# mLSTM stage of a fused kernel: a third score bank, one vector step behind each head, block maxima begun in the first stage, and no block of its own for the constants

## The reference

```python
q = layernorm(x);  k = v = ctx                          # 4 batches x 512 positions x 512
ig = cat(q,k,v) @ Wi + bi;  fg = cat(q,k,v) @ Wf + bf   # 16 gates of each kind per position
F = cumsum(log_sigmoid(fg));  log_D[s,t] = F[s] - F[t] + ig[t] for t <= s, else -inf
D = exp(log_D - rowmax(log_D))
C = (q_h @ k_h.T / sqrt(32)) * D                        # per head of 32 features, 512 x 512
h = (C / (max(|sum C|, exp(-rowmax)) + 1e-6)) @ v_h
x = x + tanh(g) * headwise_layernorm(h) * ln_scale
```

## Time and profile before

| | us |
|---|---|
| runs shown: median of 3 (lowest, highest) | 1750.79 (1750.56, 1753.29) |
| profiled execution, its own time | 1748.16 |
| its span | 1746.4 |
| PE busy in the span | 1389.4 |
| DVE busy | 1243.4 |
| ACT busy | 767.4 |
| POOL busy | 321.9 |

### The profile page before, as it was taken

How to read it: one execution, slowest core, us unless ns; L and a number is a source line. 1 busy time by engine, 2 the same in 40 slices (tenths; PEclk the granted TensorE clock), 3 DMA queues, 4 the chain that set the end, 5 groups by cost and what they waited for, 6 DMA issues and landing times. The chain is left out here.

```text
span 1746.4 us, 24792 instructions
## 1 busy us (share of the span) xinstructions
PE 1389.4 (80%) x9060; PEld 788.7 (45%) x9060; DVE 1243.4 (71%) x1952; ACT 767.4 (44%) x1450; POOL 321.9 (18%) x233
## 2 busy tenths in 40 slices
PE   3589899735568798987487696877999999999997
PEld 2367677521233344433354464533444444444443
DVE  4354666676256777895799999858778877788764
ACT  2433444335334354432688797823333333333322
POOL 0021142244555455754000000000000000000000
PEclk9777888755789899999798798989999999999998
DMA  7012133214533324222503000000000000000000
GB/s 254 3 51 71 61 121 97 73 53 149 146 101 98 117 89 129 85 98 101 200 2 120 24 0 0 0 1 4 9 6 6 6 12 6 6 6 6 12 6 12
DMA packets 56494, 102.19 MB, mean 59 GB/s; under 512 B 9823, under 2 KB 20727, under 8 KB 56300
## 3 DMA queue, kind: packets, MB, share of 16 engines
q1 hardware_dynamic: 55148, 97.14, 17.1%
q0 software_dynamic: 1280, 4.20, 0.9%
HBM read 73.47 MB, written 27.66 MB: 58 GB/s over the span
## 5 line engine op out<-in xcount | busy, mean ns | idle before, releaser
L2047 PE MATMUL HG<-W1H,XT 128*128 128x512 f16 x512 | 166.7, 388 | 27.2 <-ACT XT L2008 20.7
L1521 PE MATMUL FD<-W0D,HH 128*128 128x512 f16 x512 | 159.2, 394 | 14.6 <-DMA W0D<-down_weights,IDX 11.0
L2047 PE MATMUL HU<-W1H,XT 128*128 128x512 f16 x512 | 163.2, 380 | 0.0
L2073 PE MATMUL HD<-W1H,HT 128*128 128x512 f16 x512 | 155.3, 380 | 0.0
L1515 PE MATMUL FG<-F,W0G 97*128 97x512 f16 x324 | 84.4, 394 | 49.8 <-DMA F<-features_kept 23.3
L318 ACT ACTIVATE DD<-E,TM 128x128 f32<-128x128 f32 x256 | 72.6, 370 | 115.8 <-PE E L411 115.6
L1768 ACT ACTIVATE PR<-A_S,NM,CM 128x512 f32<-128x512 f32 x128 | 99.5, 777 | 34.4 <-DVE NM L1909 34.4
L2016 ACT ACTIVATE SG<-HG,DS 128x512 f32<-128x512 f32 x64 | 43.9, 686 | 160.3 <-PE HU L2047 160.3
L2150 DVE SCALAR_TENSOR_TENSOR H<-HU,DS,SG 128x512 f32<-128x512 f32 x64 | 48.0, 750 | 87.4 <-ACT SG L2016 85.4
L1405 POOL TENSOR_TENSOR HL<-HM,HH 128x512 f16<-128x512 f32 x64 | 92.5, 1445 | 82.6 <-ACT HH L1444 82.0
L1521 PE MATMUL FD<-W0D,HL 128*128 128x512 f16 x256 | 100.8, 394 | 0.0
(11 more groups left out here) (333 smaller groups left out, 3376.7 us busy)
## 6 DMA issues: line engine op xcount, KB each, us to landing
VALP<-in_ffn_weights_dram SPq DMA_DIRECT2D x24, 512.0 KB, 3.5
VALQ<-in_ffn_weights_dram SPq DMA_DIRECT2D x24, 512.0 KB, 3.6
quantised_weights<-QQ SPq DMA_DIRECT2D x24, 512.0 KB, 2.8
X<-in_x_dram SPq DMA_DIRECT2D x8, 1024.0 KB, 6.2
CTX<-in_ctx_dram SPq DMA_DIRECT2D x8, 1024.0 KB, 5.5
W1H<-quantised_weights SPq DMA_DIRECT2D x3, 2048.0 KB, 10.5
W1L<-quantised_weights SPq DMA_DIRECT2D x3, 2048.0 KB, 15.2
F<-features_kept SPq DMA_DIRECT2D x16, 288.0 KB
```

The lines of the kernel that those rows point to most:

```text
L1521: last = pe.matmul(DN[c][:, :], lhs[:, i, c * P:(c + 1) * P], W2[:, i, part, :], start=(i == 0 and n == 0), stop=(i == KI - 1 and n == 2))
L2047: ins = pe.matmul(bank[:, :], lhs, rhs, start=(i == 0), stop=(i == len(terms) - 1))
L2073: ins = pe.matmul(DN[0][:, :], HT[:, q, lp, k, :], W[:, 2, i * D:(i + 1) * D], start=(i == 0 and lp == 0 and W is WH), stop=(i == KI - 1 a ...
```

## The change

1. The bank T1 becomes a third score bank. Head n's scores are in QK[n % 3], and scores(pair+1) waits for the first product of the pair only. State and state read share T0, so state(n) waits for the read of the group before.
2. DVE's loop runs over heads: one product, then (second head of a group) the state read, (even heads) the addition of the pair before, and one background step. The coefficients take batch 0 and the start of batch 1, `finish` the heads 2 to 12, block maxima the heads in PEAK_HEADS.
3. Eleven of the 24 block maxima are taken in the first stage: nine behind the last normalisation, one in the wait for ACT's logarithm, one between the two subtractions of line 554 to 556. Their loads stand in SP's list ahead of the NP stores.
4. The block for the constants is gone. Its loads come behind the first load of x in SP's list, its casts behind batch 0's normalisation; WG and GLN are loaded with batch 1 and prepared behind its normalisation. MV and SD have room per batch, and ACT takes the root of the next batch ahead of a batch's copies.
5. scores(0) and two decays come ahead of state(0), and ACT's first state copy behind head 1.

```diff
+FINISH_HEADS = (2, 12)
+COEF_HEADS = (0, 1, 13, 14, 15)
+PEAKS_FIRST = 11
+PEAK_HEADS = {2: (0, 1, 4, 8, 13, 14, 15), 3: (1, 4, 8, 13, 14, 15)}
-    T = [ps("T0"), ps("T1")]
-    QK = [ps("QK0"), ps("QK1")]
+    T = [ps("T0")]
+    QK = [ps("QK0"), ps("QK1"), ps("QK2")]
...
             for b in range(B):
-                if b:
-                    sp.dma_start(X[:, b * NC:(b + 1) * NC, :], xr[b]).then_inc(x_in[b], 16)
+                sp.dma_start(X[:, b * NC:(b + 1) * NC, :], xr[b]).then_inc(x_in[b], 16)
+                if b == 0:
+                    sp.dma_start(CST[:, :], A["shape_constants"]).then_inc(consts_in, 16)
...
                 sp.dma_start(ctx_room[b], ctx[b]).then_inc(ctx_in[b], 16)
-                if b == 0:
+                if b == 1:
...
             spline.load(sp)
+            peaks.transfers(sp, 0, PEAKS_FIRST)
...
+            act.wait_ge(eps_ready, 3)
+            deviation(0)
+            act.wait_ge(consts_in, 3 * 16)
+            nc.scalar.activation(tg[:, :], tg[:, :], ACT.Tanh).then_inc(tanh_ready, 1)
             act.wait_ge(pre_pool, 3)
+            deviation(1)
             for b in range(B):
-                deviation(b)
+                if b >= 1 and b + 1 < B:
+                    deviation(b + 1)
...
             def scores(pair):
-                    pe.wait_ge(c_ready, 2 * pair)
+                    pe.wait_ge(c_ready, 2 * pair - 1)
...
             def state(n):
-                    pe.wait_ge(state_taken, n)
+                    pe.wait_ge(read_taken, n)
...
+            pe.wait_ge(tm_taken, 2)
+            scores(0)
+            decay(0)
+            decay(1)
+            pe.wait_ge(tm_taken, 5)
             state(0)
-            scores(0)
-            for n in range(4):
-                decay(n)
+            decay(2)
+            decay(3)
...
+            for n in range(PEAKS_FIRST - 2):
+                peaks.peak(v, n)
             gate_rows = CST[:, CST_W - 1:CST_W]
             v.wait_ge(t_ready, 8 * B)
...
-            for pair in range(HEADS // 2):
+            for n in range(HEADS):
+                b, h = divmod(n, NH)
+                if h == 0:
                     last_batch = finish(b - 1) if b else iter(())
+                v.wait_ge(qk_ready, n // 2 + 1)
+                v.wait_ge(d_ready, n + 1)
+                if n >= 2:
+                    v.wait_ge(pv_done, n - 1)
+                v.scalar_tensor_tensor(out=CC[:, n % 2, :], in0=QK[n % 3][:, :], scalar=DH ** -0.5,
+                                       in1=DD[:, n % 4, :], op0=ALU.mult, op1=ALU.mult).then_inc(c_ready, 1)
+                if h % HG == 1:
+                    take_read(n // HG)
+                if n % 2 == 0 and n:
+                    take_pair(n // 2 - 1)
+                if b == 0 or (b == 1 and h in COEF_HEADS):
+                    next(coefficients, None)
+                if b and FINISH_HEADS[0] <= h <= FINISH_HEADS[1]:
...
+                    next(last_batch, None)
+                if b >= 2 and h in PEAK_HEADS[b]:
+                    peaks.peak(v, peak)
```

More of the change, by code:

```diff
@@ L188, in _ @@
                     sp.dma_start(CTX[:, :, :], ctx[b + 1]).then_inc(ctx_again, 16)
-                peaks.transfers(sp, b)
                 if b == 0:
+                    peaks.transfers(sp, PEAKS_FIRST, PEAKS_FIRST + 2)
+                elif b == 1:
                     spline.store(sp)
+                else:
+                    done = PEAKS_FIRST + 2 + sum(len(PEAK_HEADS[i]) for i in range(2, b))
+                    peaks.transfers(sp, done, min(Q_TILES, done + len(PEAK_HEADS[b])))
             sp.wait_ge(pv_done, B * NH)
@@ L390, in scores @@
                         r = slice(DH * (j + jj), DH * (j + jj) + DH)
[L391 removed]
+                        last = pe.matmul(QK[(2 * pair + jj) % 3][:, c * P:(c + 1) * P], KT[r, b, g, c * P:(c + 1) * P],
                                          QT(b)[r, g, c * P:(c + 1) * P], start=True, stop=True)
@@ L469, in _ @@
                     scores(pair + 1)
-                    fill(ahead + 1)
+                fill(ahead + 1)
                 weigh(2 * pair + 1)
@@ L484, in pre, with constants, gate_weights @@
                 ins.then_inc(pre_dve, 1)
[L486 to L496, removed]
+            v.memset(EPS[:, 0:1], 1e-5).then_inc(eps_ready, 1)
+            v.memset(EPS[:, 1:2], 1.0).then_inc(eps_ready, 1)
+            v.memset(EPS[:, 2:3], 1e-6).then_inc(eps_ready, 1)
+            def constants():
+                pre(v.memset(ONE[:, :], 1.0))
+                v.wait_ge(consts_in, 3 * 16)
+                pre(v.tensor_copy(idb, idf))
+                pre(v.tensor_copy(idh, idf))
+                for c in range(NC):
+                    pre(v.tensor_copy(FUT[:, c, :], CST[:, P:2 * P]))
+                pre(v.tensor_copy(PICK[:, :], CST[:, 2 * P:2 * P + NH]))
+            def gate_weights():
+                v.wait_ge(w_loaded, 3 * 16)
+                pre(v.tensor_tensor(WG[:, 4:8, :], WG[:, 4:8, :], WG[:, 8:12, :], ALU.add))
+                v.wait_ge(tanh_ready, 1)
+                pre(v.tensor_scalar(GLN[:, :], GLN[:, :], tg[:, 0:1], -1.0, ALU.mult, ALU.mult))
+                assert n_pre[0] == PRE_DVE
             n_own = [0]
@@ L664, in _ @@
+                if b >= 2 and h in PEAK_HEADS[b]:
+                    peaks.peak(v, peak)
+                    peak += 1
+                if h == NH - 1:
                     for _ in last_batch:
                         pass
+                    if b == 1:
+                        for _ in coefficients:
+                            pass
+            assert peak == Q_TILES
             take_pair(HEADS // 2 - 1)
@@ L1156, in __init__, with transfers @@
         self.peak_ready, self.mx_ready, self.all_max = (nc.alloc_semaphore("p_" + n) for n in ("peak", "mx", "all_max"))
-    def transfers(self, sp, b):
-        for n in range(max(0, (b - 1) * PEAKS_B + 2), min(b * PEAKS_B + 2, Q_TILES)):
+    def transfers(self, sp, first, last):
+        for n in range(first, last):
             if n >= 2:
```

101 lines of the change are left out of this document (34 added, 67 removed).

## The result

| | before | after |
|---|---|---|
| median (lowest, highest), 4 runs each | 1752.04 (1750.56, 1764.51) | 1678.52 (1676.28, 1683.32) |
| profiled execution, its own time | 1748.16 | 1683.32 |
| its span | 1746.4 | 1681.5 |

The ratio is 0.9569, 95% interval 0.952 to 0.9619. The forecast was 1675 with a range of 1660 to 1708: faster, with 3.5 us too much hoped for. Of the forecast saving of 75.6 us the medians show 73.5.

A forecast was written before the change was run, and what follows sets the result against it. The prediction took TensorE's long waits in the head loop, from VectorE's order and paid twice through half clock, as the bound. Savings of 64.6 (loop), 9 (first stage) and 2 (tail) make 75.6 us: 1675, range 1660 to 1708.

The forecast's parts named there:

- The bound and the cure: Head loop: VectorE's order causes TensorE's long waits, each paid twice through half clock; respacing the steps saves 64.6 us.
- The late root: Finish's step at head 11 waits for ScalarE's root; next product 1.05 us late in three batches, 3.2 us in all.
- Fourteen groups: Head loop, fifth weigh to sixty-first: 219.67 us becomes 164.8, at 11.35 a group plus extras; saves 54.9 us.
- rival (a): Clock still drops behind late roots, in the first stage, or from steps beside GpSimd: 1690 to 1705 us; chance 0.27.
- 2.7 us for uneven groups: Allowance within the loop's fourteen groups for uneven steps and fast groups that measured up to 0.12 us longer.
- The first stage: Up to the gate product, line 529: starts at 58 in place of 66.92 us; saves 9, range 5 to 12.
- the prediction's signs: What would show it, among others: loop clock over 0.95, waits under 1.2 us, gate product (line 529) at 56 to 60.
- The start, the last group and the tail: Head loop's start, its last group, and line 570 behind it: save 1.1, 2.7 and 2 us.
- the blocks behind: The other 1377 us, behind the first 369: code unchanged, forecast saving 0.
- (b): Head loop: only half of the waits go, 7 of 14 groups at 15.7 us or more; 1705 to 1735; chance 0.08.
- (d): Loop bound by something unseen, so the change does next to nothing: within 4 us; chance 0.03.
- (c): Head loop: many short waits hold the clock down, groups about 20 us; slower, about 1800 us; chance 0.03.

The follow-up runs named there:

- e2: The changed kernel with all of VectorE's work of a pair behind the second product again, three score banks kept; 1731.50 us, ratio 0.9866.
- e7: e3 with five needless maxima on VectorE behind the third head in twelve groups of batches 1 to 3; 1720.27 us, one run.
- e1: The changed kernel with two score banks in place of three, VectorE's new order kept; 1687.11 us, ratio 0.9612.
- e10: Against a kernel with seven early maxima, half the fillers and ScalarE's next-batch root moved: finish at heads 1 to 11, its squares and root earlier; 1665.15 us, ratio 0.9495.
- e11: The changed kernel once more, nothing altered; 1678.48 us, ratio 0.9570.
- e3: The changed kernel with seven instead of nine block maxima ahead of the gates, the two others in batch 1; 1677.88 us, ratio 0.9560.
- e12: e10 with ScalarE's next-batch root ahead of a batch's copies again and all fillers in the first eight heads; 1662.77 us, ratio 0.9482.
- e6: e3 with three needless maxima on VectorE behind the third head in twelve groups of batches 1 to 3; 1683.42 us, one run.
- e4: The changed kernel without the head loop's filler matmuls, their waits kept; 1685.93 us, ratio 0.9622.
- e5: e3 with finish's step that needs ScalarE's root moved from head 11 to 12 and the last one to 13; 1682.46 us, ratio 0.9598.

## Why the prediction was right, and where it was off

**The bound and the cure: right.** The cause read from the earlier trace rows, waits that come from VectorE's order and are paid twice, is what e2 brings back and what e7 makes by hand. Clock 0.97, all waits at 1.21 or less (under 1.2 was said), free groups at 11.35 exactly: forecast and found. The third bank is worth 4 to 9 us by e1. The prediction held that the new order needs it; e1 has no wait over 1.0 us without it, so the order is only better with it.

**The late root: right in place and size.** One wait per batch behind ACT's root, forecast 1.05 each (0.95 by its own terms, 11.47 against 10.52), measured 0.78, 0.78 and 1.21; a group with one took 0.94 longer. e10, which has the root two heads earlier, doesn't have them. That the clock held behind them was in part luck: the prediction took a wait of about 1 us as harmless from one row, 220.94, and in e2 the clock fell behind three of four such waits.

**Fourteen groups: 3.4 us short.** The 51.5 hold one group of 17.2 us (120.12 - 102.89, from read to read) that rival (a) had named: a step beside GpSimd's work and a drop behind it. GpSimd copies values at that moment, in the kernel after:

```profile
103.15 1.96 POOL L216 COPY VA<-CTX 128x2048 f32<-128x2048 f32 x1
```

The step at 103.51 takes 1.88 us instead of 0.42, the product behind it is late, TensorE waits 0.77 us at 106.72, and the clock is low for ten:

```profile
110.00:118.00 8.00, 7.78 (x37) 6.58 (x36) 3.18 (x6) 1.46 (x6) 3.95 (x7) 0.50 0.01 2
...
118.50:275.00 156.50, 150.26 (x1305) 123.60 (x1325) 118.28 (x201) 86.78 (x276) 47.82 (x41) 1.00 0.23 73
```

Behind the two waits of 0.78 us and, until 275, behind that of 1.21 it stays at 1.00. In e11, the same program, GpSimd's copy runs from 102.14 to 104.10 and is over when the step starts at 104.86; the step takes 0.41 us, TensorE doesn't wait there, and the same stretch is

```profile
108.00:118.00 10.00, 10.00 (x91) 8.09 (x91) 7.14 (x16) 4.90 (x18) 5.39 (x9) 1.00 0.01 2
```

91 matmuls in ten us, and a group of 11.35. This group is worth 5.9 us from read to read (5.5 from weigh to weigh, as the table counts) and differs from one execution to the next: e11's profiled execution took 1678.13, 5.2 less than the first. The prediction's 2.7 us for uneven groups was too much for the others: of the 9.3 us over 14 x 11.35 the slow group has 5.5, the three roots 2.8 and all else 0.9. And this although product steps of `finish` beside GpSimd took 1.84 to 2.91 us in batches 1 and 2 and 1.22 in batch 3, where GpSimd is idle: the slack took most of it up.

The Trainium skill, "GPSIMD Engine Reference", section "1. Specifications", says that GpSimd's way to SBUF is shared with VectorE and that instructions with two SBUF inputs contend. The rows at 103.51 (1.88 us in place of 0.42) and 194.02 (2.91 in place of 1.22) agree: both have two inputs in SBUF, and both run beside a GpSimd instruction.

**The first stage: the term that was mis-sized.** Forecast 9, measured 5.8; the product started at 61.13, outside the 56 to 60 of the prediction's signs. Gates(0) began at 31.75 (31.8 was said) and its half clock was seen coming; the sum of the gates came at 56.29, some 2 us later than said. But the maxima set the end: the first pair was in at 40.1, not 36, the pace of 2.4 us per tile was as forecast, so the ninth ended at 60.45 and not at 56.4. Had the maxima not been there, the product could have started at 57.0; e3 shows 58.6 with a wait for ACT ahead of it, e12 56.9. The mistake was in the load's start: the first tiles stand behind x, ctx and the coefficients, and from 32 to 38 the DMA share is 0.98 to 1.04 in the kernel after, so the engines are full until then. The sum had let them run dry some 4 us too soon. The trace tells where 3 of these 4 went. The prediction had x and ctx in at about 29, with some 4 us for small rows. In the kernel after SP's list stands for 13 us in the issues of WG and GLN (2.53 from 4.73, 7.70 from 7.30, 2.88 from 15.04), the third megabyte of x is issued at 17.97 only, the DMA engines run at 0.53 from 16 to 20, and the last load of ctx lands at 19.55 + 12.8 = 32.4:

```profile
7.30 7.70 SPq L175 DMA_DIRECT2D WG<-in_L_xattn_Wf_dram  x1
...
19.55 0.71 SPq L172 DMA_DIRECT2D OUT<-in_ctx_dram  x1
```

```profile
DMA to landing us min/median/max: 12.8/12.8/12.8
```

No experiment moved WG and GLN in the list, so what that would give is not shown.

**The start, the last group and the tail** came within 1 us of their terms; line 608 (570 before) took 1.02 us at 278.38 in place of 2.59.

**What wasn't forecast: the blocks behind.** Their code is unchanged, but they took 3.7 us longer. Counted from the next block's first matmul, every kernel here takes longer than the 1377.1 of before, by 0.8 (e2) to 8.8 us (e12). It goes with how soon the first part ends, but only in part: +0.8 in e2, where it ends at 348.4, and +8.8 in e12 (277.3), yet +4.5 in e7 (336.9), +1.9 in e6 (302.6), +5.9 in e1 (300.4) and +7.3 in e4 (296.6). The time goes between that matmul and the load of ctx for the attention (453.6 us before, 456.9 after, 462.9 in e12). Why is open: no kernel here was made to tell it.

**Rivals.** Of (a) one drop happened, beside GpSimd's work, in one profiled execution of two; the late roots brought none ahead of the last group. (b) and (d) didn't. (c), many short waits that hold the clock down, didn't happen either: 0.97 over the loop. e6 tests it at one short wait in four weighs, eleven of 0.50 or 0.76 us, and has 0.99; a wait before most weighs was never made. The Trainium skill, "TensorE: Matmul & The Clock Gate", section "A second HAM failure mode: psum-queue depth-cycling", tells of such swings; the trace of the kernel after, whose 64 heads cycle through three banks, shows one drop between 88 and 268 us, and that of e12 none between 85 and 252.

## What to carry to other kernels

When the tight engine's granted clock is low, look for its longest waits first: spread the helper's long steps so that one stands behind each product that is due, and check each against the slack until the next one is due. Work that is moved into a wait must fit with its loads, not only with its own time: count their pace from the moment when the queue and the DMA engines are really free. Filler matmuls have a price once their engine is the bound, and cover too: without any the drops came back. All of them where the loop starts and half of them behind gave the lowest median (e12), though not clear of half of them throughout (e10).

## What was not expected of the hardware

- The length of a wait goes with the chance of a drop and doesn't settle it. Over all fourteen profiles, of the weighs ahead of the last group that waited over 0.3 us for their product, the clock fell during the wait or shortly behind it at 23 of 25 with 1.69 us or more, at 3 of 11 with 1.01 to 1.54, and at 9 of 33 with less. Equal waits in one execution had different sequels (0.65 in e5, 1.69 in e7, 1.01 and 1.02 in e2). Four of the nine short ones lie at the loop's start in kernels with fewer fillers, some 5 us behind a wait of 0.6 to 0.9 us for ACT, and twice in e4 the clock fell with no such wait at all. What decides isn't shown.
- A VectorE instruction with two SBUF inputs beside GpSimd: 0.42 becomes 1.88 us, 1.22 becomes 1.84 to 2.91.
- A drop lasts very unlike times: 3.4 us behind some waits of e7, ten from 107.9 on in the kernel after, 27 from 196 on in e4.
